# TensorE's program of a Mamba and gated-MLP layer with all sixteen blocks in sequence instead of a loop of eight passes

## The chip, the core and the metric

The kernel runs on one core of one Trainium2 chip. The metric is device time in microseconds (us) of one execution. The profile is that of one execution; its span runs from the first to the last instruction of the program on that core.

## The reference

The input is `u`, 2 sequences of 2048 rows of 512 numbers. One layer norm feeds two branches, and both are added to the input:

```python
x = L0_attn_u
xn = _layernorm(x, axis=-1)
x = x + _L0_attn_ref(xn, ...) + _L0_ffn_ref(xn, ...)
```

The first branch is a state-space layer. It projects `xn` to z, x, B, C and dt; puts a causal convolution over 4 rows and a silu on x; turns B and C into `elu + 1`; scans with a decay (`ssd_chunked`: within a chunk a masked product, between chunks a state); normalizes each row, multiplies by `silu(z)` and projects back to 512. The second branch is a gated MLP whose weights lie behind Hadamard transforms: `silu(x_gate) * x_up`, 2048 wide, and a projection back to 512.

## The kernel before, in words

A preparation (the first 160 us) folds the Hadamard transforms and scales into the weights. It splits each weight into a high and a low half in fp16, and lays them into the on-chip memory for good. After that no weight is loaded.

The rows are then worked in 16 **blocks** of 256 rows (`NBLOCKS`, two tiles of 128 rows, `NT`), eight for each sequence. In this text they are numbered 0 to 15. Every engine has its own program, and for one block that program is an order written out by hand, a list of short step names: `PE_STEPS` for TensorE, `DVE_STEPS`, `ACT_STEPS`, `POOL_STEPS`, and `SP_STEPS` for the queue that issues DMAs. The engines meet only through semaphores that count up over the whole program, so each wait is for a value that depends on the block's number `i`, for example `pe.wait_ge(xT_loaded, (i + 1) * 2 * NT * 16)` in line 923.

TensorE's steps of a block, in short, as they stand in `PE_STEPS`:

- `bc`, the first, projects the block's rows (`xnT`) to B, C and dt: 24 matmuls with a moving side of 144 columns, `bank<-wi,pair 128x144` in the trace. It waits for the four transposes that bring `xnT` (line 923).
- `xp0` and `xp1` follow, 24 matmuls of 256 columns each (`bank<-pair,wi`), the x part of the projection. `F0` to `F15` are up and gate of the MLP (`bank<-pair,wug`), `D0` to `D15` its projection back (`bank<-wd,h`, 6 matmuls each); `D14` waits for DVE's step `L14` (line 1244).
- `O1`, the last, projects the second tile's y back (`bank<-wo,Mx`, 24 matmuls of 512 columns). It waits for y's transposes.

Each product is three matmuls (high by high, high by low, low by high), each with its own weight load; all go through `products`, so nearly all of TensorE's work has line 912. A block has about 835 matmuls and as many weight loads.

At the end of a block the DMA queue SP issues eight transposes in a row: four of y's second tile (`yd10`, `yd11`, line 873), then four of the next block's normalized rows (`xd`, in `turn_x`, lines 265 and 266). The last of these lets the next `bc` start.

Only the numbering is a loop. Before the change TensorE runs a hardware loop (`Fori`) of eight **passes**, and each pass has two blocks written out, so blocks 0 and 1 are pass one. `j` is a register there, and `i` is worked out from it: the wait's value is put into a register ahead of the wait, which is what the instructions with line 902, 938 and the like do. A constant wait needs no register. The other engines have loops of their own (ACT and POOL over 16 blocks, DVE over 7 and over 8, SP over 14); they are the same before and after.

Of the kernel before, what the change touches and what calls it, by code (L numbers as in the profile page):

```python
# [25 lines left out]
NBLOCKS = BATCH * NBLK  # L26
# [114 lines left out]
def program(nc, u, in_w, conv_w, conv_b, a_log, dt_bias, d_param, norm_scale, out_w,  # L141
# [10 lines left out]
    with ctx:  # L152
# [115 lines left out]
        with ExitStack() as prep:  # L268
# [410 lines left out]
            def _(pe):  # L679
# [7 lines left out]
                for step in PREP_PE:  # L687
# [6 lines left out]
                    elif k == "nb":  # L694
                        if n >= 1:
                            pe.wait_ge(norms_taken, n)
                        for m, (src, _) in enumerate(NORM_BLOCKS[n], PIECE[n]):
                            pe.wait_ge(piece_squared, m + 1)
                            w = src.shape[-1]
                            nc.tensor.matmul(banks[6][:, 0:w], ones16[:, :], square[m % 8][:, 0:w],  # L700
                                             start=m == PIECE[n], stop=m == PIECE[n + 1] - 1).then_inc(piece_summed, 1)
# [191 lines left out]
        def _(pe):  # L893
# [113 lines left out]
                                 first=False, last=not down_closes(c)).then_inc(acc_filled, 1)  # L1007

            pe.sem_inc(ring_filled, NR)
            with pe.Fori(0, NBLOCKS // 2) as j:  # L1010
                body(j * 2)
                body(j * 2 + 1)

        @block.scalar
        def _(act):
# [372 lines left out]
```

## Time and profile before

| | |
|---|---|
| three runs | 1884.44, 1885.15 and 1885.6 us, median 1885.15 us |
| span of the profiled execution | 1883.3 us |
| median less that span | 1.85 us |
| first `bc` of block 0; end of the last matmul of block 15 | 163.48 us; 1876.98 us |
| TensorE (PE) matmul busy | 1808.6 us, 96% of the span |
| weight loads (PEld), DVE, ACT, POOL | 66%, 74%, 65%, 16% of the span |
| mean granted TensorE clock | 0.991 of full speed |

The profiled execution has no time of its own besides its span; what lies around a span in the timed runs is the 1.85 us in the third row of the table.

How to read the rows below: in a timeline, a row starts with the start and the length in us, then engine, line, operation, out<-in by the program's names with its shape and how many instructions were merged; in square brackets stands the idle time of the engine before it and what ended it. "issue" means that the engine waited for nothing that the profile shows. PEldq is TensorE's sequencer, the part that reads instructions and executes register operations and branches itself. SPq is the DMA queue. A granted clock of 1.00 is 2.4 GHz, 0.50 is 1.2 GHz.

### The profile page before, as it was taken

What the parts mean: (1) busy time and instruction counts of PE and PEld (TensorE: products, weight loads), DVE (VectorE), ACT (ScalarE), POOL (GpSimd) and SP (SyncE); (2) the same over time, 40 slices, a digit from 0 to 9 for tenths busy, and PEclk for the clock granted to TensorE, in tenths of its full rate; (3) what the DMA queues carried; (4) which work ended last, traced back from release to release, by engine and by line L of the source; (5) the groups of instructions that cost most, each with busy time, mean ns of one, the idle gap of its engine ahead of it and who ended that gap; (6) DMA issues with size and microseconds to landing.
All of it is one profiled execution on the core that took longest, in us unless ns stands there. A gap on an engine that the chain in (4) does not pass through costs nothing.

```text
span 1883.3 us, 40159 instructions
## 1 busy us (share of the span) xinstructions
PE 1808.6 (96%) x13745; PEld 1244.5 (66%) x13746; DVE 1387.9 (74%) x2859; ACT 1228.6 (65%) x2583; POOL 308.9 (16%) x270
## 2 busy tenths in 40 slices
PE   5779999999999999999999999999999999999998
PEld 2346767576776767576766768677675757666674
DVE  6986867768585877758585877858686786848686
ACT  7957848476665848566574848556583857658483
POOL 0000202112030202103030211203020211203020
PEclk9989999999999999999999999999999999999999
DMA  8212122221312222121312222121312312131222
GB/s 320 71 65 57 47 57 80 46 71 34 79 43 75 62 57 79 32 71 44 81 46 58 79 46 74 37 72 46 88 49 57 79 32 82 34 80 46 61 75 57
DMA packets 217544, 125.60 MB, mean 67 GB/s; under 512 B 179662, under 2 KB 180790, under 8 KB 216886
## 3 DMA queue, kind: packets, MB, share of 16 engines
q1 hardware_dynamic: 216870, 122.30, 24.0%
q8 instruction: 129, 2.11, 0.5%
q10 hardware_dynamic: 528, 1.05, 0.2%
q14 instruction: 17, 0.14, 0.0%
HBM read 72.18 MB, written 8.65 MB: 43 GB/s over the span
## 4 chain that ended last, share of the span: by engine, by line
PE 80%; DVE 10%; issue 3%; DVEq 2%; SPq 2%; ACT 1%; DMA 1%; ACTq 0%
PE bank L912 78%; SPq L873 1%; DVE pair L228 1%; DVE pair L230 1%; DVEq L1287 1%; DVE wi L666 1%; DVEq L1312 1%; DVE v L1289 1%; DVE Mx L1271 1%; DVE wug L624 1%; PE bank L728 0%; PE bank L732 0%; DMA wi<-n_L_attn_out_proj_w_dram 0%; PE bank L729 0%; DVE pair L223 0%
## 5 line engine op out<-in xcount | busy, mean ns | idle before, releaser
L912 PE MATMUL bank<-pair,wug 128*128 128x256 f16 x6144 | 699.8, 273 | 0.0
L912 PEld LDWEIGHTS bank<-pair,wug 128*128 128x128 f16 x6144 | 596.3, 98 | 90.3 <-issue 3.4
L912 PE MATMUL bank<-wd,h 128*128 128x512 f16 x1536 | 360.4, 379 | 1.8 <-DVE h L1244 1.6
L1186 POOL TENSOR_TENSOR state<-state,dec 128x512 f32<-128x512 f32 x64 | 80.0, 1260 | 1104.1 <-ACT neg L1101 830.7
L1233 DVE SCALAR_TENSOR_TENSOR pair<-pair,conv 128x256 f32<-128x256 f32 x384 | 180.1, 513 | 105.5 <-ACT pair L1049 94.8
L912 PEld LDWEIGHTS bank<-wd,h 128*128 128x128 f16 x1536 | 148.0, 98 | 165.4 <-DVE h L1244 5.1
L912 PE MATMUL bank<-wi,pair 128*128 128x512 f16 (+1 forms) x1152 | 200.3, 328 | 3.6 <-DVEq L1346 3.0
L912 PE MATMUL bank<-pair,wi 128*128 128x256 f16 x1536 | 183.8, 282 | 18.9 <-issue 18.9
L912 PEld LDWEIGHTS bank<-pair,wi 128*128 128x128 f16 x1536 | 154.7, 101 | 41.9 <-issue 20.1
L1115 ACT ACTIVATE Mx<-Mx,cs_own 128x128 f32<-128x128 f32 x512 | 162.2, 387 | 6.3 <-DMA Mx<-cs_rows 5.9
L912 PEld LDWEIGHTS bank<-wi,pair 128*128 128x128 f16 x1152 | 99.6, 98 | 100.0 <-DVEq L1346 3.8
L1174 POOL TENSOR_TENSOR pair<-v 128x512 f32<-128x512 f16 x64 | 86.7, 1354 | 426.3 <-DMA v<-pair 377.1
L1266 DVE TENSOR_TENSOR Mx<-Mx,Gm 128x512 f32<-128x512 f32 x128 | 111.6, 872 | 38.4 <-ACT Mx L1119 24.4
L1064 ACT ACTIVATE pair<-bank,gate_scale 128x256 f32<-128x256 f32 x128 | 60.4, 472 | 75.9 <-PE bank L912 54.8
L1093 ACT ACTIVATE stateK<-state 128x512 f16<-128x512 f32 x64 | 39.7, 620 | 82.5 <-DVE state L1298 82.5
L1064 ACT ACTIVATE tg<-bank,gate_scale 128x256 f32<-128x256 f32 x128 | 59.9, 468 | 50.8 <-PE bank L912 49.0
L1298 DVE SCALAR_TENSOR_TENSOR state<-bank,state 128x512 f32<-128x512 f32 x64 | 43.8, 684 | 63.8 <-PE bank L912 63.8
L1240 DVE SCALAR_TENSOR_TENSOR tg<-tg,h_scale,bank 128x256 f32<-128x256 f32 x128 | 60.8, 475 | 40.1 <-ACT tg L1064 34.2
L1271 DVE TENSOR_TENSOR Mx<-Mx 128x512 f16<-128x512 f32 x96 | 78.3, 815 | 10.8 <-ACT Mx L1130 9.1
L1119 ACT ACTIVATE Mx<-Mx 128x512 f32<-128x512 f32 x128 | 80.6, 630 | 8.1
L912 PE MATMUL bank<-wo,yT 128*128 128x512 f16 x384 | 85.5, 379 | 0.0
L912 PE MATMUL bank<-wo,Mx 128*128 128x512 f16 x384 | 85.5, 379 | 0.0
(253 smaller groups left out, 2716.0 us busy)
## 6 DMA issues: line engine op xcount, KB each, us to landing
Mx<-cs_rows SPq DMA_DIRECT2D x128, 256.0 KB, 3.6
pair<-in_L_attn_u_dram SPq DMA_DIRECT2D x17, 512.0 KB, 3.3
Mx<-in_L_attn_u_dram SPq DMA_DIRECT2D x16, 512.0 KB, 3.6
out_dram<-Mx SPq DMA_DIRECT2D x16, 512.0 KB, 2.8
big<-in_L_ffn_W_down_dram SPq DMA_DIRECT2D x2, 2048.0 KB, 16.8
wug<-in_L_attn_in_proj_w_dram SPq DMA_DIRECT2D x2, 2048.0 KB, 12.6
pair<-in_L_ffn_W_gate_dram SPq DMA_DIRECT2D x4, 1024.0 KB, 5.3
pair<-in_L_ffn_W_up_dram SPq DMA_DIRECT2D x3, 1024.0 KB, 15.5
```

Source lines behind the costliest of these rows:

```text
L912: ins = nc.tensor.matmul(out, lhsT, rhs, start=first and n == 0, stop=last and n == len(pairs) - 1)
L1064: nc.scalar.activation(tg[c % 2][:, :], ug[c % 2][:, 0:TB], ACT.Silu, scale=gate_scale[:, c:c + 1]).then_inc(gate_ready, 1)
L1093: nc.scalar.activation(stateK[:, hf * 512:(hf + 1) * 512], state[:, hf * 512:(hf + 1) * 512], ACT.Copy, scale=1.0 / LOW).then_inc(state_hi ...
L1115: nc.scalar.activation(M[q][:, n, :], M[q][:, n, :], ACT.Relu, scale=-1.0, bias=cs_own[:, c, 4 * q + n:4 * q + n + 1])
L1119: nc.scalar.activation(M[q][:, :, :], M[q][:, :, :], ACT.Exp, scale=-1.0).then_inc(M_exp, 1)
L1174: pool.tensor_tensor(by_tile(vd[:, :]), v16[:, 4 * hf:4 * hf + 4, c, 0, :], v16[:, 4 * hf:4 * hf + 4, c, 1, :], ALU.add)
L1186: pool.tensor_tensor(half, half, bcast(dec3[:, 2, c, 8 * hf:8 * hf + 8], HD), ALU.mult).then_inc(state_faded, 1)
L1233: ins = nc.vector.scalar_tensor_tensor(cv[n % 2][:, c, :], x[:, c, j:j + TB], conv[:, CX * j + t:CX * j + t + 1], cv[n % 2][:, c, :], ALU. ...
L1240: nc.vector.scalar_tensor_tensor(tg[c % 2][:, :], tg[c % 2][:, :], h_scale[:, c:c + 1], ug[c % 2][:, TB:2 * TB], ALU.mult, ALU.mult).then_ ...
L1266: nc.vector.tensor_tensor(M[q][:, :, :], M[q][:, :, :], Gm[:, c, :].unsqueeze(1).to_broadcast([P, 4, P]), ALU.mult).then_inc(M_whole, 1)
L1271: nc.vector.tensor_tensor(M_lo[q], M[q][:, :, :], M_hi[q], ALU.subtract).then_inc(M_ready, 1)
L1298: nc.vector.scalar_tensor_tensor(half, o[:, :], 1.0 / PEAK, half, ALU.mult, ALU.add).then_inc(dve_emptied, 1)
```

## The change

The loop of eight passes with two blocks each becomes a Python loop over the 16 blocks that writes all of them out. `i` is then a number and no register, and the values of all TensorE's waits become constants.

```diff
             pe.sem_inc(ring_filled, NR)
-            with pe.Fori(0, NBLOCKS // 2) as j:
-                body(j * 2)
-                body(j * 2 + 1)
+            for j in range(NBLOCKS):
+                body(j)
```

No matmul is added, removed or reordered. Two places show what moves, both in TensorE's order. The names are those of the trace, and in square brackets stand the semaphores that an instruction waits for.

The first is the entry to block 0, behind the preparation's last Hadamard products. Before:

```order
L732 MATMUL bank<-wt,had 128x512 [waits wt_copied,hw_stored] x3
L892 UNCONDITIONAL_BRANCH
L1010 UNCONDITIONAL_BRANCH [waits prepared]
L1010 ISA
L902 ISA [waits xT_loaded]
L912 MATMUL bank<-wi,pair 128x144 [waits dve_emptied]
L912 MATMUL bank<-wi,pair 128x144 x23
L902 ISA
L912 MATMUL bank<-pair,wi 128x256 [waits act_emptied]
```

And with the change:

```order
L732 MATMUL bank<-wt,had 128x512 [waits wt_copied,hw_stored] x3
L892 UNCONDITIONAL_BRANCH
L912 MATMUL bank<-wi,pair 128x144 [waits prepared,dve_emptied,xT_loaded]
L912 MATMUL bank<-wi,pair 128x144 x23
L912 MATMUL bank<-pair,wi 128x256 [waits act_emptied]
```

The loop's entry and the register instructions (ISA, REGISTER_ALU) between the groups of matmuls are gone, and the waits stand on the matmuls.

The second is the end of a pass, from the last `D` step of its second block on (`bank<-wd,h`). Before, the compare-and-branch goes back to the row `L902 ISA [waits xT_loaded]` above, or leaves the loop:

```order
L945 REGISTER_ALU
L912 MATMUL bank<-wd,h 128x512 [waits h_ready]
L912 MATMUL bank<-wd,h 128x512 x5
L912 MATMUL bank<-wo,Mx 128x512 [waits yT_loaded1]
L912 MATMUL bank<-wo,Mx 128x512 x23
L1010 REGISTER_ALU
L1010 COMPARE_AND_BRANCH
```

With the change, at this place as at the end of every other block:

```order
L912 MATMUL bank<-wd,h 128x512 [waits h_ready]
L912 MATMUL bank<-wd,h 128x512 x5
L912 MATMUL bank<-wo,Mx 128x512 [waits yT_loaded1]
L912 MATMUL bank<-wo,Mx 128x512 x23
L912 MATMUL bank<-wi,pair 128x144 [waits dve_emptied,xT_loaded]
L912 MATMUL bank<-wi,pair 128x144 x23
L912 MATMUL bank<-pair,wi 128x256 [waits act_emptied]
```

`O1` is followed at once by the next block's `bc`; no branch stands between them.

## Rows read from the trace of the kernel before

**Rows 1.** The profile page: span; busy time, share and instructions of each engine.

```profile
span 1883.3 us, 40159 instructions
...
PE 1808.6 (96%) x13745; PEld 1244.5 (66%) x13746; DVE 1387.9 (74%) x2859; ACT 1228.6 (65%) x2583; POOL 308.9 (16%) x270
```

**Rows 2.** TensorE's waits: what it waited for, us in total, times, longest us.

```profile
PE bank L912 <- issue: 18.9, 7, 2.9
...
PE bank L912 <- DVEq L1346: 3.0, 1, 3.0
...
PE bank L912 <- DVE h L1244: 1.6, 5, 0.4
...
PE bank L912 <- DMA pair<-pair: 0.5, 2, 0.3
```

**Rows 3.** The loop's line 1010: duration ns min/median/max, first and last start us.

```profile
L1010 PEldq COMPARE_BRANCH  x8: 83/3540/3869, 370.1 to 1873.0; - x8
```

**Rows 4.** Timeline of TensorE, end of block 7 and start of block 8.

```profile
1017.14 1.67 PE L912 MATMUL bank<-wi,pair 128*128 128x144 f16 x24
1018.65 0.27 PE L912 MATMUL bank<-pair,wi 128*128 128x256 f16 x1
1021.62 6.96 PE L912 MATMUL bank<-pair,wi 128*128 128x256 f16 x47 [2.70 <-issue]
```

**Rows 5.** The same timeline from block 8 to block 9, inside a pass.

```profile
1126.62 1.66 PE L912 MATMUL bank<-wi,pair 128*128 128x144 f16 x24
1128.12 5.40 PE L912 MATMUL bank<-pair,wi 128*128 128x256 f16 x48
```

**Rows 6.** Blocks as windows: length, PE busy (matmuls), granted clock, DMA share, GB/s; all sixteen summed.

```profile
163.48:268.39 104.91, 104.91 (x834) 1.00 0.21 57
268.39:374.24 105.85, 105.24 (x836) 1.00 0.22 56
374.24:482.21 107.97, 105.21 (x834) 1.00 0.24 63
...
587.69:697.10 109.41, 106.66 (x835) 0.98 0.23 62
...
911.95:1017.14 105.19, 105.09 (x835) 1.00 0.23 57
...
1126.62:1232.08 105.46, 105.16 (x836) 1.00 0.24 57
1232.08:1341.72 109.64, 106.76 (x835) 0.98 0.24 63
...
1662.07:1771.46 109.39, 106.77 (x835) 0.98 0.23 63
...
sum 1713.50, PE 1692.20; mean PE 105.76
```

**Rows 7.** The same view of the stretches behind two stalls, of blocks 8 and 2.

```profile
1021.90:1025.30 3.40, 3.40 (x18) 0.50 0.43 159
...
376.00:381.00 5.00, 2.24 (x22) 1.00 0.26 95
```

**Rows 8.** The same view summed over blocks 1, 3, ... 13, then over blocks 2, 4, ... 14.

```profile
sum 738.40, PE 736.30; mean PE 105.19
...
sum 764.67, PE 745.76; mean PE 106.54
```

**Rows 9.** Who ended the idle time before line 1204, DVE's first step of a block: us, times.

```profile
  PE bank L912: 86.8, 15
```

**Rows 10.** DMA queues inside block 9, 1126.7 to 1232.0 us: packets, MB, share.

```profile
q8 instruction: 8, 0.13, 0.5%
```

**Rows 11.** The same view of 1003.5 to 1017.1 us, the end of block 7.

```profile
q8 instruction: 2, 0.03, 0.9%
```

**Rows 12.** SP's timeline: the last transpose before block 8, and before block 9.

```profile
1013.78 2.07 SPq L266 DMA_TRANSPOSE pair<-pair  x1
...
1122.58 1.26 SPq L266 DMA_TRANSPOSE pair<-pair  x1
```

## The prediction

> **What bounds the kernel now.** I read the page first: PE is busy 96% of the span and the next engine, DVE, 74% [rows 1]. So the question is what PE's own time holds besides matmuls at full pace. The waits of TensorE answer it: in the blocks it waits 18.9 us for "issue", in 7 pieces of up to 2.9 us, and hardly at all for others: 1.6 us for DVE at `D14`, 0.5 us for the transposes [rows 2]. Seven is the number of times that a loop of eight passes goes back. The loop's own line says the same from the sequencer's side: of 8 compare-and-branches the last, not taken, took 83 ns; the median is 3540 ns and the longest 3869 ns [rows 3].
>
> The timeline shows where it hurts. Inside a pass, from block 8 to block 9, `bc` and the 48 matmuls of `xp0` and `xp1` follow without a gap, the 48 in 5.40 us [rows 5]. At the loop's return, from block 7 to block 8, `bc` starts on time, one matmul of `xp0` follows, and then PE stands still for 2.70 us; the other 47 take 6.96 us [rows 4]. So a return costs in two ways: the stall, and slower matmuls behind it. The windows name the second: 3.4 us behind the stall have a granted clock of 0.50, which is 1.2 GHz, where it was 1.00, or 2.4 GHz, through block 7, before the engine stood idle [rows 6, 7].
>
> The windows by block put a price on it all [rows 6]. Block 0, where nothing is waited for, takes 104.91 us and PE is busy for all of it. The second blocks of the passes, behind no return, take 105.19 to 105.85 us. The blocks behind a return (2, 4, ... 14) take 107.97 to 109.64 us. Block 2 is the shortest of them, and its clock stayed at 1.00 after the stall [rows 6, 7]; for the other six, from block 4 to block 14, it is 0.98 over the block.
>
> **The change part by part.** *The seven taken branches go.* With them go the 18.9 us of stall [rows 2]. The sequencer's own 3.5 us per branch are hidden today: the branch is executed while the array still works through queued matmuls of `O1`, and `bc` then starts on time. That cover is not needed any more.
>
> *The clock.* Six windows at 0.50 for 3.4 us each do half the columns, so each loses 1.7 us; block 8's 47 matmuls bear this out (6.96 us, against 47/48 of 5.40, 5.29 us). 6 x 1.7 = 10.2 us. The sums agree roughly: PE is busy 745.76 us in blocks 2 to 14 and 736.30 us in blocks 1 to 13, for the same matmuls [rows 8]. Without the idle time before it I expect no fall: in the blocks without a stall the clock is 1.00 [rows 6].
>
> *The register instructions go.* They are executed by the sequencer ahead of the array. Block 0 has them all, and PE is busy for 104.91 of its 104.91 us. So they are worth nothing, and I bound them by 0 on both sides. The loop's entry before block 0 lies in the 3.0 us that PE waits there for DVE to end the preparation [rows 2], and is worth nothing either.
>
> *What is late next.* A stall of 2.7 us also gave the others time. Blocks without a return behind them show what PE waits for when it isn't held up: DVE's `L14` before `D14` (up to 0.4 us) and the transposes before `bc` (up to 0.3 us) [rows 2]. Blocks 1, 3, ... 13 are therefore my model of every block after the change. Their lengths add up to 738.40 us, 105.49 us each; blocks 2, 4, ... 14 add up to 764.67 us, 109.24 us each [rows 8]. If the latter become like the former, 764.67 - 738.40 = 26.3 us go. By terms: 18.9 + 10.2 = 29.1 us, less what these seven blocks now have in hand: stripped of stall and clock they take (764.67 - 29.1) / 7 = 105.08 us, 0.41 us less than the model, and 7 x 0.41 = 2.9 us is given back. Both ways give 26.2 to 26.3 us.
>
> *The ends of blocks 1, 3, ... 13* still hold something of the loop: the branch stands between `O1` and `bc`, and two instruction fetches run beside the transposes there [rows 11]. The last of the eight takes 2.07 us to issue before block 8 and 1.26 us before block 9 [rows 12]. What that is worth in the block's length shows in no row by itself. At worst it is nothing: block 9 has 8 fetches in 105.3 us [rows 10], about one in the 13.6 us of such an end, so the two that the model bears are no less than what a straight program brings. At best it is all that the model block has above block 0, 0.58 us, for 14 block ends 8.1 us. I take 0.1 us for each of the 14, 1.4 us, near the lower end, since `D14`'s wait is most of that 0.58 and stays.
>
> Sum: 26.3 + 1.4 = 27.7 us off a span of 1883.3 us, 1855.6 us. The median of the runs stood 1.85 us above that span; nothing of the change lies outside the span, so I add it again: **1857.4 us**.
>
> *The fetch of a longer program.* The written-out program must be fetched from memory. So must today's: one stretch of 105.3 us inside a pass (block 9) holds 8 instruction fetches, 0.13 MB [rows 10], and in it PE is busy 105.16 of 105.46 us [rows 6]. A straight program is fetched ahead without a wait, and the new one is straight throughout. I cost it at nothing. If a fetch did stall the engine, the price would be that of a return: 2.7 us, and 1.7 us more if the clock falls.
>
> **The rivals.** *Every block like block 0.* If `D14`'s wait and the late transposes come from the loop too (its fetches falling on DMAs that others wait for), blocks 1 to 15 all take 104.91 us. Then the blocks' sum falls from 1713.5 to 16 x 104.91 = 1678.6 us: 34.9 us less, 1850.3 us. For it: fetches do lie beside those transposes, and they are slower there [rows 11, 12]. Against: DVE's own work leads up to `D14`, and block 0 lacks DVE's sum of the block before.
>
> *The others take over.* Today an unhindered block is always followed by one with a rest of 4.4 us. Without it DVE, ACT or the chain of transposes could fall behind from block to block. All blocks would be 105.85 us, as block 1 is, or more. At 105.85 for blocks 1 to 15 the gain is 1713.5 - 104.91 - 15 x 105.85 = 20.8 us, 1864.3 us; from 1.9 us over the model per block on (26.3 / 14), the gain is gone and the time 1885 us. Against it: DVE stands idle before its first step of nearly every block, 86.8 us over 15 blocks, 5.8 us each [rows 9], so lateness doesn't pass from one block to the next. It would have to use up those 5.8 us first.
>
> *Slower: fetches that come too late.* Should the straight program cross into instructions not fetched yet, it would stall in the middle of a block as it does now after a return. It decides at 6.3 such stalls of 2.7 + 1.7 us: 27.7 us. At eight crossings in each of 16 blocks, all stalling, it would be 128 x 4.4 = 563 us more than the 1857.4; at one in a block 16 x 4.4 = 70 us, 1928 us. For it: at a return the stall comes 25 matmuls behind the branch's own 3.5 us [rows 3, 4], so a fetch that isn't ahead costs several us. Against it: 8 fetches in block 9 and PE busy all but 0.3 us of it [rows 10, 6].
>
> *The branch isn't the cause.* Were a taken branch no dearer than the one that wasn't taken, 83 ns [rows 3], and the stalls due to something else at the blocks' start, such as DMAs or waits, then only 7 x 0.083 = 0.6 us would go, 1884.6 us. Against it: blocks 1, 3, ... 15 start with the same steps, and where such a start is shown it has no stall [rows 5]; and the 18.9 us come in just 7 pieces [rows 2]. A rule of the Trainium skill takes this rival's side: "Advanced Engine Details and Errata", section "Control Flow Timing", gives a compare-and-branch about 108 ns, by which an estimate for seven is 0.76 us and the change nothing that can be told. By that rule, the trace agrees for the branch not taken (83 ns) and disagrees for the others, whose median is over thirty times as long [rows 3].
>
> **How the numbers follow.** The forecast (all blocks between 105.0 and 105.85 us) has a chance of 0.80, every block like block 0 0.08, the others taking over in part (1864.5 to 1881 us) 0.05 and fully (1885 us) 0.02, a branch that isn't the cause (1884.6 us) 0.02, late fetches 0.03. The range goes from the block-0 case, 1850 us, to all blocks like block 1, 1864.5 us: 0.88 of the chance by these cases, of which I keep some back for what I haven't thought of. About 0.2% (3.8 us) can be told from no change. Faster takes the first three, 0.80 + 0.08 + 0.05 = 0.93; same the next two, 0.04; slower the last, 0.03.
>
> **What would show it.** In the profile after, line 1010 has no branch; PE's waits have no "issue" piece of 2 us within the blocks; the clock is 1.00 from the first `bc` to the last matmul; all windows from one `bc` to the next are 104.9 to 105.9 us; the instruction queue still fetches some 8 times per block; DVE waits some 5.8 us before line 1204's successor. I am wrong if "issue" waits stay at new places (fetch), or if blocks are longer than 105.9 us with waits for DVE or DMAs at `D14` or `bc` (the others take over).

## The result, and the profile after

The changed kernel takes 1856.04 us (median of four runs, 1854.08 to 1857.09), the kernel before 1884.8 us beside it. The ratio is 0.985, with a 95% interval of 0.9836 to 0.9863. The forecast was 1857.4 us, in a range of 1850.0 to 1864.5. The profiled execution has a span of 1855.1 us, where 1855.6 was forecast. It was the slowest of the four: its time is 1857.09 us, 1.99 above its span, so the median stands only 0.94 us above that span, not 1.85.

The page's first lines answer to [rows 1]. PE is busy 7.7 us less for the same 13745 matmuls, so they ran at a quicker pace on the mean.

```profile
span 1855.1 us, 39438 instructions
...
PE 1800.9 (97%) x13745; PEld 1242.1 (67%) x13746; DVE 1386.6 (75%) x2859; ACT 1226.6 (66%) x2583; POOL 307.1 (17%) x270
```

TensorE's waits, against [rows 2]. Lines after 1010 carry a number one lower than before. "issue" and the transposes have left the list; the entry into block 0 is as it was; DVE's wait has grown from 1.6 to 3.0 us. The description of the kernel, the prediction and the expectations call the step that waits there `D14`, and DVE's step `L14`. In the traces they are `D12` and `L12`: the wait lies ahead of the six matmuls between `F15` and `O0`. From here on it is called `D12`; where an expectation says D14, the same wait is meant.

```profile
PE bank L912 <- DVEq L1345: 3.1, 1, 3.1
PE bank L912 <- DVE h L1243: 3.0, 7, 0.6
```

TensorE's timeline from block 7 to block 8, the place of [rows 4]. It now reads like the inside of a pass in [rows 5]: 48 matmuls in 5.40 us, with no gap.

```profile
1007.83 1.66 PE L912 MATMUL bank<-wi,pair 128*128 128x144 f16 x24
1009.33 5.40 PE L912 MATMUL bank<-pair,wi 128*128 128x256 f16 x48
```

The blocks as windows, with the columns of [rows 6]: block 0, block 2 (once behind a return), block 3, block 5, block 8 (once behind a return), and the sum of all sixteen. The last row is the stretch behind the start of block 0.

```profile
163.73:270.27 106.54, 106.54 (x834) 0.98 0.23 55
...
375.93:480.98 105.05, 105.05 (x835) 1.00 0.24 63
480.98:586.46 105.48, 105.07 (x835) 1.00 0.23 59
...
692.08:797.13 105.05, 105.05 (x836) 1.00 0.23 58
...
1007.83:1113.26 105.43, 105.07 (x835) 1.00 0.24 59
...
sum 1685.47, PE 1682.35; mean PE 105.15
...
164.30:167.70 3.40, 3.40 (x26) 0.51 0.02 5
```

The sum of the blocks was 1713.50 us and is 1685.47: 28.0 us less, against 28.2 us of the span. Blocks 2 to 14 are no longer the long ones. Every block after block 0 takes 104.93 to 105.66 us, and there are two kinds: those like block 5, in which PE is busy throughout, and those like block 3, in which it stands still for about 0.4 us. Block 0 is a surprise: its clock is at 0.51, the 1.2 GHz level, for 3.4 us, where it was 1.00 before.

Three more rows: SP's last transpose before block 8, against [rows 12]; the fetches in block 9, against [rows 10]; and what ends DVE's idle time before its first step, now line 1203, against [rows 9].

```profile
1003.79 1.26 SPq L266 DMA_TRANSPOSE pair<-pair  x1
```

```profile
q8 instruction: 6, 0.10, 0.4%
```

```profile
  PE bank L912: 86.2, 16
```

The transpose no longer takes 2.07 us. A block holds 6 or 7 fetches. DVE still stands idle for 5.4 us on average before its first step of a block, so it has not become the bound.

### The profile page after: what moved, and what is told of

Same layout as the page of the kernel before. It is cut to its first block, busy times and chain, and to the rows that moved or that the text cites. A ratio compares the mean times of both kernels' runs of the same rounds, so it can differ in the third digit from the quotient of the medians.

```text
span 1855.1 us, 39438 instructions
## 1 busy us (share of the span) xinstructions
PE 1800.9 (97%) x13745; PEld 1242.1 (67%) x13746; DVE 1386.6 (75%) x2859; ACT 1226.6 (66%) x2583; POOL 307.1 (17%) x270
## 3 DMA queue, kind: packets, MB, share of 16 engines
q8 instruction: 109, 1.79, 0.4%
## 4 chain that ended last, share of the span: by engine, by line
PE 79%; DVE 11%; DVEq 3%; issue 2%; ACT 1%; DMA 1%; SPq 1%; ACTq 0%
PE bank L912 77%; DVE pair L228 1%; DVE pair L230 1%; DMA big<-in_L_ffn_W_down_dram 1%; DVEq L1286 1%; DVE v L1288 1%; DVEq L1311 1%; DVE wug L624 1%; DVE wi L666 1%; DVE Mx L1270 1%; PE bank L728 1%; DVE vw L1301 0%; DVE pair L223 0%; PE bank L729 0%; DVE pair L1279 0%
## 5 line engine op out<-in xcount | busy, mean ns | idle before, releaser
L912 PE MATMUL bank<-pair,wi 128*128 128x256 f16 x1536 | 173.7, 273 | 0.0
L912 PEld LDWEIGHTS bank<-pair,wi 128*128 128x128 f16 x1536 | 150.2, 98 | 17.3
L1092 ACT ACTIVATE stateK<-state 128x512 f16<-128x512 f32 x64 | 39.7, 620 | 82.5 <-DVE state L1297 82.5
L1239 DVE SCALAR_TENSOR_TENSOR tg<-tg,h_scale,bank 128x256 f32<-128x256 f32 x128 | 60.9, 476 | 40.1 <-ACT tg L1063 34.2
```

The source lines that it names most:

```text
L912: ins = nc.tensor.matmul(out, lhsT, rhs, start=first and n == 0, stop=last and n == len(pairs) - 1)
L1092: nc.scalar.activation(stateK[:, hf * 512:(hf + 1) * 512], state[:, hf * 512:(hf + 1) * 512], ACT.Copy, scale=1.0 / LOW).then_inc(state_hi ...
L1239: nc.vector.scalar_tensor_tensor(tg[c % 2][:, :], tg[c % 2][:, :], h_scale[:, c:c + 1], ug[c % 2][:, TB:2 * TB], ALU.mult, ALU.mult).then_ ...
```

## The experiments

Two questions were open. What makes a return cost something: the branch itself, or the instructions that must be fetched? And why do some blocks still wait 0.4 us at `D12`? Each run was compared with the kernel before on the same chip, which took 1880.96 to 1883.26 us in these groups, so the ratios are what to compare. In the diffs `-` and `+` are against the kernel before in the first four and in the two passes, and against the changed kernel where `body(j)` stands alone. In these edits a "slot" is a place in a stretch of 256 instructions, counted from 0. The profiles bear this size out: the changed kernel's 109 fetches (1.79 MB, 16 KB each) go with 13745 matmuls and 13746 weight loads on TensorE, 252 for each fetch, and some waits beside them.

### Twice as many returns

```diff
-            with pe.Fori(0, NBLOCKS // 2) as j:
-                body(j * 2)
-                body(j * 2 + 1)
+            with pe.Fori(0, NBLOCKS) as j:
+                body(j)
```

> The loop has one block per pass, sixteen passes, so 15 returns where there were 7; the register waits are as many as before. If the price is per return (28.8 us for 7, so 4.1 us each), the time is 1856 + 15 x 4.1 = 1918 us, with 15 issue waits of 2.5 to 2.9 us. If it is the register waits that cost, the time stays at that of the kernel before, 1885 us.

Measured: 1891.18 us, ratio 1.0054 (1.0031 to 1.0077). Slower, but by far less than seven returns had cost. This is well below the 1918 us expected for a price per return. First its "issue" waits, then its timeline at one of the returns:

```profile
PE bank L912 <- issue: 26.1, 15, 2.3
```

```profile
1237.17 0.27 PE L912 MATMUL bank<-pair,wi 128*128 128x256 f16 x1
1239.23 5.29 PE L912 MATMUL bank<-pair,wi 128*128 128x256 f16 x47 [1.79 <-issue]
```

There are 15 stalls, as expected, but of 0.97 to 2.34 us, 1.74 on average instead of 2.7. The clock fell behind only three of them (2.07, 2.07 and 2.34 us long; a third of 2.07 us left it at 1.00). Behind this one of 1.79 us the 47 matmuls take 5.29 us, the full pace. So a return has no fixed price. It costs its stall, and the clock only sometimes. Why the stalls are shorter here is read below, with the head at slot 230.

### The loop kept, its head moved to slot 0

```diff
-            with pe.Fori(0, NBLOCKS // 2) as j:
+            with nc.Fori(0, NBLOCKS // 2, engines=[pe.engine], head_slot={pe.engine: 0}) as j:
```

> The loop of eight passes is kept as before; only its first instruction is moved to slot 0 of a 256-instruction fetch block (by padding ahead of the loop). Fetch theory: the sequencer then has a whole fetched block behind the return, 256 instructions or over 10 us of array work, and the next block arrives in that time; no issue wait above 0.5 us, no fall of the clock, 1855 to 1860 us, with the seven taken branches still there at about 3.5 us each on the sequencer. Rival (a taken branch costs the array 2.7 us and a clock wherever its target lies): 1885 us.

Measured: 1853.51 us, ratio 0.9842 (0.9826 to 0.9859). In the order of the fences: the branch's row, TensorE's waits, its timeline at the return before block 8, and the sixteen blocks as one window.

```profile
L1010 PEldq COMPARE_BRANCH  x9: 83/3830/4047, 160.9 to 1842.6; - x9
```

```profile
PE bank L912 <- DMA pair<-pair: 1.4, 5, 0.4
PE bank L912 <- DVE h L1244: 0.2, 1, 0.2
```

```profile
1005.59 1.67 PE L912 MATMUL bank<-wi,pair 128*128 128x144 f16 x24
1007.09 5.40 PE L912 MATMUL bank<-pair,wi 128*128 128x256 f16 x48
```

```profile
162.05:1846.51 1684.46, 1682.71 (x13344) 1.00 0.24 61
```

The loop is still there, and its branches take as long as ever (the ninth is one at the entry). But no "issue" wait is left, and the ratio is that of the written-out program within the intervals. So the branch as such doesn't stall PE. At five of the seven returns `bc` still waits 0.2 to 0.4 us for its transposes, 1.4 us in all, and at the other two, of which the one shown is one, for nothing. In the kernel before, the loop's head lay some 55 instructions ahead of the end of its fetched stretch: `bc`, one matmul of `xp0`, a weight load for each, and a few register instructions. PE ran these and then stood still until the *next* stretch had arrived. With the head at slot 0 there are 256 instructions to work on while it comes. The Trainium skill, "Runtime: NRT & Kernel Launch", section "Instruction fetch mechanics", says that instructions come in blocks of 256, that straight code is fetched ahead, and that a taken branch out of the window forces a fetch; the trace agrees with its 3.8 us branches and 16 KB fetches, and adds that the block behind the target decided the stall here.

### The head at slot 230

The same edit with `head_slot={pe.engine: 230}`, so that only 26 instructions lie ahead of the end.

> The same loop, its first instruction at slot 230, so that only 26 instructions lie between the return and the end of the fetch block, where I estimate some 55 in the kernel before (the stall comes after 25 matmuls and 26 weight loads). Fetch theory: the stall moves forward into bc, to about the 10th or 11th matmul, and gets longer by the array work that no longer covers it, some 1 us: issue waits of 3.2 to 4 us, 1885 to 1893 us. Rival (the stall belongs to the branch or to the steps at a block's start): it stays behind the 25th matmul at 2.7 us, 1885 us.

Measured: 1881.64 us, ratio 0.9995 (0.9981 to 1.0008). TensorE's timeline at the return before block 8, and its waits:

```profile
1016.31 0.92 PE L912 MATMUL bank<-wi,pair 128*128 128x144 f16 x12
1020.04 0.92 PE L912 MATMUL bank<-wi,pair 128*128 128x144 f16 x12 [2.81 <-issue]
```

```profile
PE bank L912 <- issue: 19.3, 7, 2.9
```

The stall has moved to the middle of `bc`, behind 12 matmuls with their 12 weight loads: the place follows the end of the fetched stretch. Its length did not grow as I expected. The reason is when the next fetch begins: 1.2 to 1.4 us after `bc` here, 2.0 to 2.3 us after it in the kernel before, and 0.4 to 1.8 us after it with sixteen passes. In all 30 stalls of the kernel before, of sixteen passes, of two passes (below) and of slot 230, PE goes on 2.2 to 2.6 us behind the start of that fetch. So it is this fetch that ends the stall; why it begins at different times is open. The time is below the 1885 to 1893 us expected, since the stalls didn't grow. The clock fell behind six of the seven stalls.

### A hint ahead of the branch

```diff
-            with pe.Fori(0, NBLOCKS // 2) as j:
+            with nc.Fori(0, NBLOCKS // 2, engines=[pe.engine], hint_back_edge=True) as j:
```

Measured: 1857.49 us, ratio 0.9867 (0.985 to 0.9883). The branch and the hint among the sequencer's rows, then TensorE's waits:

```profile
L1010 PEldq COMPARE_BRANCH  x8: 88/357/389, 368.9 to 1844.3; - x8
L1010 PEldq BRANCH_PREFETCH_HINT  x8: 36/36/45, 159.2 to 1634.2; - x8
```

```profile
PE bank L912 <- DVE h L1244: 3.1, 8, 0.6
```

A return now takes 357 ns instead of 3540, and no "issue" wait is left. The ratio is that of the written-out program within the intervals. The profile has 122 fetches, 129 in the kernel before: seven fewer, one for each return. It would fit that the hint has the target's stretch fetched in place of the one behind the loop's end, so that the next stretch too comes earlier; this isn't shown. That makes two ways of keeping the loop and losing its price.

### Two passes of eight blocks

```diff
-            with pe.Fori(0, NBLOCKS // 2) as j:
-                body(j * 2)
-                body(j * 2 + 1)
+            with pe.Fori(0, 2) as j:
+                for n in range(NBLOCKS // 2):
+                    body(j * (NBLOCKS // 2) + n)
```

> The loop has two passes of eight blocks: one return, and the register instructions and register waits in every block as before the change. Fetch theory: 1.5 to 2.9 us of stall and perhaps 1.7 us of clock for the one return, else the changed kernel's 1856 us: 1857 to 1861 us. Rival (the register instructions and waits carry the gain): near 1885 us.

Measured: 1857.05 us, ratio 0.987 (0.9846 to 0.9894). TensorE's waits:

```profile
PE bank L912 <- issue: 1.5, 1, 1.5
```

All register instructions ahead of the waits are still executed, and one return is left. The time is that of the changed kernel, run again in a later group at ratio 0.987. So the register instructions are worth nothing that can be told within these intervals, about 4 us, and the gain is that of the stalls and the clock.

### Where in a block the fetches fall

In the changed kernel's trace, blocks 1, 3, 4, 6, 8, 11, 13 and 15 have a fetch that begins 33.5 to 39.8 us after the block's start. The seven waits at `D12`, 0.29 to 0.58 us long, are in the first seven of these, and block 15 alone has none that is listed. In the other eight blocks no fetch begins then; theirs come at 24.1 to 29.9 and next at 42.9 to 47.0 us, and `D12` doesn't wait. In the kernel before, all odd blocks had a fetch 33.3 to 33.8 us in, and the five waits [rows 2] were in odd blocks. That stretch of a block is when SP issues four transposes of `v` for POOL. What a fetch delays is their landing. Here is the last of the four in block 4, with a fetch, and in block 5, without one (issues in the DMA view: count, us from issue to landing):

```profile
v<-pair SPq DMA_TRANSPOSE x1, 4.5
...
v<-pair SPq DMA_TRANSPOSE x1, 2.5
```

This holds for all: the last of the four lands 40.0 to 41.9 us into the eight blocks with such a fetch, and 39.7 to 39.9 us into the other seven behind block 0. Block 3 (with a fetch) and block 5 (without) show what happens, first in SP's timeline, then in POOL's, DVE's and PE's; block 3 starts at 480.98 us and block 5 at 692.08.

```profile
514.42 1.70 SPq L867 DMA_TRANSPOSE v<-vw  x1
...
725.52 1.19 SPq L867 DMA_TRANSPOSE v<-vw  x1
```

```profile
521.67 1.53 POOL L1173 TENSOR_TENSOR pair<-v 128x512 f32<-128x512 f16 x1 [24.00 <-DMA v<-pair]
...
524.61 1.04 POOL L1178 TENSOR_TENSOR pair<-pair,row 128x512 f32<-128x512 f32 x1
...
732.25 1.15 POOL L1173 TENSOR_TENSOR pair<-v 128x512 f32<-128x512 f16 x1 [23.49 <-DMA v<-pair]
```

```profile
521.50 0.69 DVE L1270 TENSOR_TENSOR Mx<-Mx 128x512 f16<-128x512 f32 x1 [0.56 <-ACT Mx L1129]
...
523.99 0.48 DVE L1239 SCALAR_TENSOR_TENSOR pair<-pair,h_scale,bank 128x256 f32<-128x256 f32 x1 [0.25 <-ACT pair L1063]
...
524.88 1.32 DVE L1270 TENSOR_TENSOR Mx<-Mx 128x512 f16<-128x512 f32 x1
526.12 0.68 DVE L1279 TENSOR_TENSOR pair<-bank,dec 128x512 f32<-128x512 f32 x1
...
732.60 1.36 DVE L1270 TENSOR_TENSOR Mx<-Mx 128x512 f16<-128x512 f32 x1 [0.56 <-ACT Mx L1129]
...
736.11 0.74 DVE L1270 TENSOR_TENSOR Mx<-Mx 128x512 f16<-128x512 f32 x1
736.78 0.68 DVE L1279 TENSOR_TENSOR pair<-bank,dec 128x512 f32<-128x512 f32 x1
```

```profile
570.26 1.47 PE L912 MATMUL bank<-wd,h 128*128 128x512 f16 x6 [0.41 <-DVE h L1243]
```

Both transposes begin 33.44 us into their block. The one beside the fetch takes 0.51 us more, and POOL starts 0.52 us later in its block (40.69 against 40.17 us). So POOL's steps lie beside other steps of DVE. In block 5 the DVE step of line 1270 that starts 0.35 us behind POOL's is the long one (1.36 us), and DVE makes it up, since in block 3 it stands waiting for ACT at that point (0.25 us). In block 3 it is the next step of that line that is long, 1.32 us instead of 0.74, and behind it DVE waits for nobody. Its step of line 1279 starts 45.14 us into the block, against 44.70. This 0.44 us stays until `D12`, where PE waits 0.41 us. That POOL's step is what lengthens DVE's is only seen in this timing; no run separates it.

Two pairs of runs test the rest: every block of the written-out program is given the same place in the fetched stretches, once so that no fetch falls into that stretch (slot 176), once so that one does in every block (slot 83). The first pair pads with instructions that are executed.

```diff
             for j in range(NBLOCKS):
+                pe.addr_align(256, offset=176)
                 body(j)
```

> The changed kernel with padding ahead of every block, so that each starts at slot 176 of a fetch block and all sixteen fetch their instructions at the same times. Collision theory: in the changed kernel D14 waits in the eight blocks that fetch between 33 and 40 us after their start, and in no other; by its trace, a start at 176 should put the fetches near 1.5, 15, 29 and 45 us. Then no block waits at D14, all take 104.9 to 105.1 us, D14's 3.0 us of waits go and the time is 1849 to 1853 us. Rival (D14's wait is DVE's own work and falls as it will): about half of the blocks still wait, 1856 us plus some 0 to 3 us of padding.

> The same padding with every block starting at slot 83, which should put the fetches near 6.5, 20.5, 36.5 and 50 us in every block. Collision theory: every block waits at D14 for 0.2 to 0.6 us, blocks take 105.2 to 105.7 us and the time is 1856 to 1861 us, 5 to 9 us above the start at 176. Rival (D14's wait is DVE's own): no difference between the two starts.

Measured: 1956.64 us at slot 176, ratio 1.0402 (1.0381 to 1.0424), and 1963.75 us at slot 83, ratio 1.0438 (1.0416 to 1.046). For slot 176, TensorE's waits, a block's start in its timeline and the padding's row; for slot 83, one row of the waits:

```profile
PE bank L912 <- issue: 75.6, 16, 19.0
```

```profile
508.35 3.04 PE L912 MATMUL bank<-wi,pair 128*128 128x144 f16 x24 [3.77 <-issue]
```

```profile
L1011 PEldq NOP  x1821: 13/13/13, 159.1 to 1839.5; - x183
```

```profile
PE bank L912 <- DVE h L1244: 6.0, 14, 0.7
```

Both are 4% slower, which was not expected. The padding is the reason: 106 NOPs stand ahead of each block at slot 176, one every 71 ns, 7.5 us in all. They empty the queue of matmuls, PE stands still for 3.77 us ahead of each block but the first (19.0 us there, behind 231 NOPs), and the clock falls behind it. For `D12` the pair does show the expected: 0.2 us of waits in one block at slot 176, 6.0 us in fourteen at slot 83. The second pair jumps over its padding.

```diff
             for j in range(NBLOCKS):
+                pe.addr_align(256, offset=176, max_nops=0)
                 body(j)
```

> As e5, every block of the written-out program starts at slot 176, but the padding is jumped over by one branch and not executed, so e5's issue waits of 3.8 us (106 padding instructions of 71 ns each) should go. Collision theory: no block waits at D14 (as in e5, one of 16 there), all blocks 104.9 to 105.2 us, 1849 to 1854 us, some 3 us below the changed kernel. Rival (D14's wait comes from the lack of e5's rest of 3.8 us at a block's start): about half of the blocks wait, 1856 us. Should the jump cost a fetch, issue waits appear at the blocks' starts.

> As e8 with slot 83. Here the jump crosses into the next fetch block. Collision theory: D14 waits in nearly every block (14 of 16 in e6), 0.2 to 0.7 us each, blocks 105.2 to 105.7 us, 1856 to 1862 us, 5 to 9 us above e8. Rival (D14's wait is DVE's own): no difference from e8 except what a jump across a boundary costs, which shows as issue waits at the blocks' starts.

Measured: 1852.32 us at slot 176, ratio 0.9851 (0.9832 to 0.987), and 1859.93 us at slot 83, ratio 0.9893 (0.9874 to 0.9912). Slot 176, in its waits, its windows (block 2) and SP's timeline:

```profile
PE bank L912 <- DVE h L1244: 0.2, 1, 0.2
```

```profile
373.95:478.99 105.04, 105.04 (x836) 1.00 0.25 60
```

```profile
515.10 1.19 SPq L867 DMA_TRANSPOSE v<-vw  x1
```

Slot 83, the same three views:

```profile
PE bank L912 <- DVE h L1244: 6.1, 15, 0.7
```

```profile
374.52:480.02 105.50, 105.08 (x835) 1.00 0.25 61
```

```profile
516.15 2.13 SPq L867 DMA_TRANSPOSE v<-vw  x1
```

Neither has an "issue" wait. PE is busy equally long in the two blocks, and the only thing that was moved is where the fetches fall: at slot 83 this transpose takes 2.13 us instead of 1.19 (it is long in ten of the sixteen blocks), the last of the four lands 40.3 to 41.0 us into blocks 1 to 15 instead of 39.7 to 40.1, `D12` waits 6.1 us in all instead of 0.2, and the time is 7.6 us longer. So the fetches do set `D12`'s wait. The waits listed, 6.1 less 0.2, account for 5.9 us. With the pieces too short to be listed, the stretch from `F15` to `O0`, in which `D12` lies, is longer by 7.2 us in all, and the blocks' ends by 0.8: at slot 83 a fetch also begins some 103 us into each block, beside the transposes there.

### The three best, side by side

The changed kernel, slot 176 with the jump, and the loop with its head at slot 0, once more in one group.

> The changed kernel itself, for a comparison on one chip with e11 and e12: about 0.985 of the kernel before, with D14's waits in the blocks that fetch 33 to 40 us after their start (eight of sixteen, 3.0 us in all).

> e8's kernel. Collision theory: its blocks add up to 1681.6 us in e8 and to 1685.5 us in the changed kernel, so it should be 3 to 4 us below e10, ratio to the kernel before about 0.983. If the difference lies in the chips of the two calls, it equals e10 within 1 us.

> e2's kernel, the loop kept with its head at slot 0. Its blocks add up to 1684.5 us in e2, so 0.5 to 1.5 us below e10 and 2 to 3 us above e11; the loop costs nothing that a written-out program saves. If a loop's return still cost something unseen, it would be slower than e10.

Measured: 1856.66, 1851.53 and 1853.35 us, with ratios of 0.987 (0.985 to 0.9889), 0.9846 (0.983 to 0.9862) and 0.9855 (0.9836 to 0.9873). The waits of the changed kernel in this group:

```profile
PE bank L912 <- DVE h L1243: 2.9, 8, 0.7
```

In the other two the same row is 0.2 us, in one block. Slot 176 is 5.1 us below the changed kernel; in the traces the blocks add up to 4.4 us less, 3.7 of it from `F15` to `O0` and 0.6 at the blocks' ends. The loop with its head at slot 0 is 3.3 us below, more than I expected of it. In both its runs the fetches of blocks 0 to 7 come at 24 to 29 us and then at 40 to 46 us, so they too keep clear of that stretch, which is worth 3.6 us; the blocks' ends lose 0.8 us against the changed kernel here, where they had lost 2.2 in the earlier run. The intervals of the three ratios overlap, so the order among them rests on the medians of one group and on the waits, and each pair is only a few us apart. All three are faster than the kernel before.

## Why the prediction was right

TensorE's timelines of the two kernels can be compared step by step, by the starts of the groups of matmuls. Outside four places the steps of the sixteen blocks take the same time in both, 1425.0 us in all. These four make up the whole 28.0 us: 29.8 - 1.3 + 1.1 - 1.6.

**The stall (18.9 us) and the clock (10.2 us).** Both went, whole. No "issue" wait is left, and blocks 2 to 14 run at 1.00. From the first matmul of `xp0` to that of `F0` the seven blocks took 66.5 us in all and now take 36.7: 29.8 us less, where the two terms add up to 29.1, so the clock was worth a little more, 10.9 us. In substance the cause was also right, a return whose instructions come late, but not quite as the text had it: the taken branch can stay. It is the stretch behind its target that was late, as the head at slot 0 and at slot 230 show.

**What the seven blocks give back (2.9 us).** Too large: the stretch from `F15` to `O0`, in which `D12` lies, grew by 1.3 us over the sixteen blocks. The model was that each becomes like its odd neighbour, with that wait. But blocks 2, 10, 12 and 14 have none. Seven of the sixteen wait, and which ones is set by the place of the fetches, not by the loop's parity.

**The block ends (1.4 us).** About right: from `O1`'s first matmul to the next `bc` the sixteen blocks took 84.4 us and now take 83.3, 1.1 less. `O1` of block 13 before and of block 7 after:

```profile
1656.45 5.34 PE L912 MATMUL bank<-wo,Mx 128*128 128x512 f16 x24
...
1002.65 5.34 PE L912 MATMUL bank<-wo,Mx 128*128 128x512 f16 x24
```

The next `bc` starts at 1662.07 us and at 1007.83 us, 5.62 and 5.18 us behind these. The 1.1 us hold the 0.5 us of waits for the transposes [rows 2], both of which lay at returns, ahead of blocks 2 and 14. The reason given for a low value was misread, though: `D12`'s wait isn't most of the 0.58 us that the model block has above block 0. In blocks 1, 3, ... 13 it adds up to 1.3 us, 0.19 us each.

**What had no term.** Block 0's clock, at 0.51 for 3.4 us, cost 1.6 us (106.54 against 104.91), against the forecast of 1.00 from the first `bc` on. PE waits 3.0 or 3.1 us ahead of block 0 in every kernel but the two with executed padding. The clock then fell in both profiles of the changed kernel, but also with the loop kept (head at 0, at 230, the hint, two passes) and with padding jumped over; it didn't in the kernel before or with sixteen passes, of which there is one profile each. So it isn't due to writing out the blocks; what sets it is open.

That the span came within 0.5 us of its forecast is in part luck: 1.6 us too much for what is given back stands against 1.6 us for block 0 that had no term. The 1.85 us added for the median were 0.94. That is scatter among the four runs, each of which took 1.98 or 1.99 us more than its own span.

**The fetch and the registers, costed at nothing.** Right: no "issue" wait in straight code, and the two passes keep the registers at the same time.

**The rivals.** *Every block like block 0* had the right suspicion, fetches falling on DMAs that others wait for, but they don't come from the loop: straight code has them as well. Slot 176 is where nearly all blocks become so, 104.91 to 105.09 us in blocks 2 to 15, and it ends at 1852.3 us. *The others take over*: no; the longest block after block 0 is 105.66 us and DVE still idles 5.4 us a block. *Late fetches*: none in straight code. The runs with executed padding do show the price of an empty queue, 3.77 us ahead of 15 blocks, and the clock behind it. *The branch isn't the cause*: for the time this was wrong. For the mechanism there is something in it, since a taken branch of 3.8 us costs nothing where it is covered.

## What to carry to other kernels

Where TensorE waits for "issue" just behind a loop's return, count the instructions from the loop's head to the stall: if their number stays the same at each return, the next stretch of instructions may be what comes late, and moving the head shows it. Here a moved head, or a hint ahead of the branch, gained as much as writing out the loop. Instruction fetches are DMA traffic: look where in a block they fall, since one beside a transpose that somebody waits for cost up to 0.7 us in a block here. Padding that is executed wasn't free on an engine that must be kept fed: it cost 4%.

## What the runs showed of the hardware that I had not expected

- A taken branch of 3.8 us on TensorE's sequencer can cost nothing, and the stall comes later, when the fetched stretch ends: behind 25 matmuls with the head some 55 instructions ahead of that end, behind 12 with 26, never with 256. It ended 2.2 to 2.6 us behind the start of the next fetch in all 30 stalls. With the hint the branch takes 357 ns.
- The price of a stall through the clock isn't proportional to it. Those of up to 1.8 us left the clock at 1.00, and of those of 2.07 to 2.9 us most, but not all, were followed by 0.50: block 2 of the kernel before kept 1.00 behind 2.76 us [rows 6, 7].
- One 16 KB fetch delays a DMA transpose beside it: in the changed kernel's eight blocks at least one of the four landed 2.6 to 4.5 us after its issue, where 2.4 or 2.5 us is usual; its row in SP's timeline grew only in some of them. By the timing, the delay reaches TensorE through POOL and DVE some 50 us later, and with a fetch there in every block the time was 7.6 us longer.
- Executed NOPs follow each other at 71 ns on TensorE's sequencer (106 of them ahead of a block), though each shows only 13 ns in its row.
